# A four-layer transformer on one core: the second and third layer as one job of a sequence, with the orders planned anew

## The chip, the cores and the metric

The kernel runs on 1 core of one Trainium2 chip. The metric is the device time of one execution in microseconds (us). The core has five engines that work beside each other and wait for one another by semaphores: TensorE (PE, matmuls), VectorE (DVE), ScalarE (ACT), GpSimd (POOL) and SyncE (SP, here only the issuer of transfers).

## The reference, cut to what matters

Input x has 16 sequences of 256 tokens, 256 features, in float32. It passes through four layers, each with its own weights and its own modulation by a conditioning vector:

```
x = L0(x, cond, ctx)   # self-attention (rope, mask), cross-attention, mlp
x = L1(x, ctx, cond)   # cross-attention alone
x = L2(x, cond, ctx)   # self-attention, cross-attention, mlp
x = L3(x, cond, ctx)   # self-attention (rope), cross-attention, mlp
```

A block normalises x, modulates it, does its work and adds the result to x. Attention has 16 heads of 16 features; cross-attention looks at 77 context tokens. An mlp goes from 256 to 1024 features and back with a gelu between (tanh form in L0 and L2, erf form in L3). Sequences do not touch each other.

## The kernel before, in words

A *job* is one sequence in one entry of the list `LAYERS` (line 65). Before, the list has four entries: L0, L1, L2, L3, so 64 jobs. All 16 jobs of an entry come before those of the next (`JOBS`, line 97). That makes passes over the sequences: in between, x lies in a DRAM tensor, x_scratch. The step `stx` stores it at a job's end (line 1117), the step `ldx` loads it at the start of the same sequence's job in the next pass (line 1027) into one of two tiles x_in.

Six jobs are in flight (`SLOTS`, line 33). Each has its own tiles x, xhat (the normalised x) and xnT (its transpose). The rest is shared in small rings: 4 PSUM banks `gen`, 2 double banks `score`, 4 tiles of probabilities, 3 for cross-attention's keys and values, and so on. Weights lie in four areas A, B, C, M; an area is loaded anew (`ldw`) when the last job that uses it has finished. L1 and L3's self-attention share area C, whose query and output weights lie in the mask tiles maskk and maskq of L0: on PE, a matmul with `maskq,xnT` in these layers is the output projection, one with `xnT,maskk` the query projection, and `ctxT,w_kvC` L1's keys. The mlps of L0, L2 and L3 share area M (w_w1M for the up-projection, w_w2M for the down-projection).

A block is cut into steps, each of which belongs to one engine. In an attention block: `ln`, `rs`, `nx` (norm: DVE, POOL, DVE), `xT` (transpose on PE, line 1213), `xe` (ACT, line 1429), the projections `qkv` (PE, lines 1204 and 1238), splitting into a high and a low part and a trip through DRAM that lays queries and keys out (DVE, ACT, SP), the scores by rows `S` (PE, lines 1266 and 1280) whose row maxima `mr` DVE takes (line 1671), the scores by columns `ST` (PE, lines 1296 and 1302) whose exponentials `ex` ACT takes (line 1489), the weighing `W` (PE, line 1322), its copy (ACT), the sums' inverse `dv` and the division `nm` (DVE, POOL line 1531), `out` (PE, line 1204) and the residual `res` (DVE). An mlp has `up` (PE, line 1342), the gelu `ge` (ACT, line 1513) and `down` (PE, line 1351). The gelu and the exponential need different tables in ACT, which are loaded at each change between the two.

The order of every engine's steps is set before the program is built: `Program.run` plays the steps through with a table of costs and picks, for a free engine, the startable step with the smallest key

```
AGE * st.job - st.rank - STAY * (same tile shape on PE as the step before) - FIRST.get(st.name, 0.0)
```

so `FIRST` (line 106) holds for each kind of step by how much it is preferred, and `STAY` how much PE keeps to one shape of tile. The engines then run these orders as written; only semaphores hold them up.

Of the kernel before, what the change touches and what calls it, by code (L numbers as in the profile page):

```python
# [14 lines left out]
B, S, D = 16, 256, 256  # L15
# [34 lines left out]
class Block:  # L50
# [3 lines left out]
    def __init__(self, of, kind, area, eps, mod=None, rope=None, mask=False, gate=None, qk_bias=None, out_bias=False,  # L54
# [11 lines left out]
    [Block("L0", "self", "A", 1e-5, mod=0, rope=P, mask=True, gate=0),  # L66
     Block("L0", "cross", "B", 1e-5, mod=1, gate=1, mask=True, ctx="raw"),
     Block("L0", "mlp", "M", 1e-5, mod=2, gate=2, out_bias=True, gelu="tanh")],
    [Block("L1", "cross", "C", 1e-5, mod=3, qk_bias=0, out_bias=True, ctx="norm", ctx_mod=4, behind=(0, 0))],
    [Block("L2", "self", "A", 1e-6, mod=5, qk_bias=2, out_bias=True, gate=3),  # L70
     Block("L2", "cross", "B", 1e-6, qk_bias=4, out_bias=True, ctx="norm"),
     Block("L2", "mlp", "M", 1e-6, mod=6, gate=4, out_bias=True, gelu="tanh")],
    [Block("L3", "self", "C", 1e-5, mod=7, rope=S),
# [29 lines left out]
HOP = {"pe": 0.29, "act": 0.21, "dve": 0.14, "pool": 0.12, "sp": 0.1}  # L103
TABLE = 1.28
TRANSFERS = ("ldx", "ldc", "ldg", "stx", "zq", "sm", "sd", "sg", "sh", "ldw", "ph", "pw", "lh", "ll", "la", "ms")
FIRST = {"ce": 15.3, "dv": 0.7, "ex": -9.3, "ge": 5.3, "hi": 11.9, "ldc": 8.9, "ldg": 13.3, "ldx": 13.4, "lh": -6.3, "ln": -5.3, "lo": 0.5, "mr": 2.3, "out": 3.8, "ph": -2.2, "pv": -6.8, "pw": 2.6, "qkv": -6.1, "rp": -8.7, "rt": -6.9, "sd": -0.6, "stx": 4.2, "up": -1.9, "ve": -10.0, "xT": -2.5, "xe": 8.2, "zq": 13.4}
MARGIN, AGE, STAY = 1.4, 16, 4
ISSUE = {"ldw": 2.5, "la": 0.5, "ms": 0.4, "zq": 0.55, "lh": 1.27, "ll": 0.63, "sm": 0.56, "sd": 0.53, "sg": 1.08, "sh": 0.53}
TILES = {"S": "rows", "ST": "rows", "W": "columns"}
SWITCH = {("whole", "rows"): 0.095, ("rows", "whole"): 0.095, ("rows", "columns"): 0.095, ("columns", "rows"): 0.1,  # L110
# [114 lines left out]
class Program:  # L225
# [154 lines left out]
    def run(self):  # L380
# [45 lines left out]
        while left:  # L426
            started = False
            for eng in ENGINES:
# [3 lines left out]
                if not can:  # L432
                    continue
                st = min(can, key=lambda st: (AGE * st.job - st.rank - STAY * (eng == "pe" and TILES.get(st.name, "whole") == self.tiles) - FIRST.get(st.name, 0.0), 0))
                could[eng].remove(st)
# [1405 lines left out]
```

How the kernel before makes its waits and increments, by code:

```python
                @block.sync  # L711
# [9 lines left out]
                                sp.dma_start(dst, src).then_inc(w_loaded[st.blk.area], 16)  # L721
                        elif st.early:
                            buf = st.got["x_in"]
                            sp.dma_start(x_in[buf][:, :, :], a["x"][st.seq].rearrange("(c p) d -> p c d", p=P)).then_inc(x_loaded[buf], 16)
                    sp.dma_start(late_gates[:, :], a["gate_bias"][0, GATES_EARLY * D:N_GATE * D].partition_broadcast(B)).then_inc(late_bias_loaded, 16)
                    sp.wait_ge(hot_ready, 1)
                    sp.dma_start(zeros_dram, zero[:, :]).then_inc(hot_placed, 16)
                    for t in k_self:
                        sp.dma_start(t[0:P:4, :, :].bitcast(F32), hot[:, :, :]).then_inc(hot_placed, 16)
                    for t in k_cross:
                        sp.dma_start(t[0:P:4, :, :].bitcast(F32), hot[:, :, 0:CTXP]).then_inc(hot_placed, 16)
                    for i, late in enumerate(LATE):
                        if late.then is None:
                            dst, src = late_dma(i)
                            sp.dma_start(dst, src).then_inc(late_loaded[i], 16)
                    sp.wait_ge(hot_placed, 16 * (1 + OWN + CROSS))
                    sp.wait_ge(gates_ready, 2)
                    sp.dma_start(gates_dram[:, 0:GATES_EARLY * D], gates[:, :]).then_inc(gates_stored, 16)
                    sp.wait_ge(gates_stored, 16)
```

## Time and profile before

| what | value |
|---|---|
| median of 3 runs | 2713.38 us (2712.58 to 2728.46) |
| the profiled execution | 2724.64 us |
| its span, first to last instruction | 2722.9 us |
| mean granted clock of PE | 0.961 |
| PE busy | 2592.7 us (95%) |
| DVE busy | 1772.4 us (65%) |
| ACT busy | 1510.7 us (55%) |
| POOL busy | 658.4 us (24%) |

The span counts from the first to the last instruction of the profiled execution. Busy time is the union of an engine's instructions; PE's matmuls overlap each other, so the durations of single matmuls add up to more than it. The granted clock of a stretch is a mean: PE's clock has a full and a half level.

### The profile page before, as it was taken

Reading aid. Unit: us, or ns where it says so; the run is one execution under the profiler, and the core shown is the slowest. Engines: PE = TensorE matmul, PEld = TensorE weight load, DVE = VectorE, ACT = ScalarE, POOL = GpSimd, SP = SyncE. Lnnn points to the kernel's source line nnn. Section 1 sums busy time; section 2 is a strip of 40 time slices with the busy share of each in tenths; the row PEclk is TensorE's granted clock in tenths of the full one; section 3 lists DMA queues with packets and bytes.
Section 4 is the critical chain, followed back from the end, with each engine's and each line's share of the span. In section 5 each row is a group of like instructions: output and inputs, shape, how many; then the busy total and the mean of one; then the engine's idle time right before and its main releaser. Section 6 shows DMA issues by size and latency. Waiting matters only on the chain.

```text
span 2722.9 us, 55574 instructions
## 1 busy us (share of the span) xinstructions
PE 2592.7 (95%) x19774; PEld 1871.0 (69%) x19774; DVE 1772.4 (65%) x4435; ACT 1510.7 (55%) x2471; POOL 658.4 (24%) x650
## 2 busy tenths in 40 slices
PE   7789999999999999989999999999999999999987
PEld 5557777777776766656677777776776777777766
DVE  4467656755765565777675767675776777677741
ACT  1335566566565554445666666655655555655562
POOL 2013212212222222212222222222332232323220
PEclk9889999999999987888999999999999999999988
DMA  6344334334334454545343434343334343434310
GB/s 201 117 132 131 117 103 146 101 103 139 108 102 131 150 183 138 175 159 166 109 153 102 146 114 148 113 142 112 116 118 153 101 144 98 135 108 147 94 62 16
DMA packets 317577, 342.69 MB, mean 126 GB/s; under 512 B 90874, under 2 KB 208474, under 8 KB 316988
## 3 DMA queue, kind: packets, MB, share of 16 engines
q1 hardware_dynamic: 284860, 292.06, 34.5%
q10 hardware_dynamic: 32256, 47.07, 4.8%
q8 instruction: 165, 2.70, 0.4%
q14 instruction: 104, 0.85, 0.1%
q0 software_dynamic: 192, 0.01, 0.0%
HBM read 203.42 MB, written 118.31 MB: 118 GB/s over the span
## 4 chain that ended last, share of the span: by engine, by line
PE 76%; DVE 12%; SPq 3%; issue 3%; DMA 3%; ACT 2%; POOL 0%; ACTq 0%; DVEq 0%; POOLq 0%
PE gen L1342 12%; PE gen L1351 11%; PE gen L1238 11%; PE gen L1204 11%; PE gen L1322 10%; DVE row_max L1671 5%; PE score L1296 4%; PE score L1251 3%; PE score L1280 3%; PE score L1266 3%; PE score L1302 3%; PE gen L1213 3%; DVE xhat L1586 1%; DVE max_tok L1686 1%; DVE stats L1574 1%
## 5 line engine op out<-in xcount | busy, mean ns | idle before, releaser
L1489 ACT ACTIVATE probs<-score 128x1024 f32<-128x1024 f32 (+1 forms) x576 | 572.3, 1027 | 331.0 <-PE score L1296 216.1
L1671 DVE TENSOR_REDUCE row_max<-score 128x4 f32<-128x1024 f32 (+1 forms) x640 | 648.5, 1044 | 139.8 <-PE score L1280 95.6
L1342 PE MATMUL gen<-xnT,w_w1M 128*128 128x256 f32 x1536 | 374.3, 393 | 2.2 <-ACT xnT L1429 2.2
L1351 PE MATMUL gen<-w_w2M,hT 128*128 128x256 f32 x1536 | 354.7, 385 | 3.0 <-ACT hT L1513 3.0
L1342 PEld LDWEIGHTS gen<-xnT,w_w1M 128*128 128x128 f32 x1536 | 284.9, 193 | 65.1 <-issue 18.2
L1351 PEld LDWEIGHTS gen<-w_w2M,hT 128*128 128x128 f32 x1536 | 286.5, 191 | 56.9 <-issue 18.3
L1523 POOL TENSOR_TENSOR rstd<-var_eps,minus_half 128x2 f32<-128x2 f32 x160 | 112.4, 703 | 864.2 <-DVE var_eps L1580 863.9
L1531 POOL TENSOR_TENSOR xnT<-xnT,xhat 128x512 f32<-128x512 f32 x112 | 142.5, 1272 | 597.0 <-DVE xhat L1700 578.3
L1498 ACT COPY oT<-gen 128x512 f32<-128x512 f32 x224 | 132.0, 589 | 218.6 <-PE gen L1322 210.8
L1429 ACT ACTIVATE xnT<-gen,mod_all 128x256 f32<-128x256 f32 x288 | 147.0, 568 | 181.3 <-PE gen L1213 180.0
L1720 DVE TENSOR_TENSOR xhat<-gen,gate 128x256 f32<-128x256 f32 (+1 forms) x112 | 60.1, 537 | 228.0 <-PE gen L1351 154.8
L1322 PE MATMUL gen<-probs,v_self 128*32 128x256 f32 x3072 | 206.1, 386 | 0.1
L1513 ACT ACTIVATE hT<-gen,b_b 128x256 f32<-128x256 f32 x384 | 159.0, 473 | 79.2 <-PE gen L1342 78.2
L1266 PE MATMUL score<-k_self,q_stack 64*128 64x256 f32 x1536 | 185.2, 335 | 12.4 <-DVE row_max L1671 8.2
L1537 POOL TENSOR_TENSOR parts<-parts,sinT 128x512 f32<-128x512 f32 (+1 forms) x96 | 109.8, 1144 | 346.3 <-DVE parts L1615 346.3
L1296 PE MATMUL score<-q_stack,k_self 64*128 64x256 f32 x1536 | 183.5, 336 | 0.8 <-ACT probs L1489 0.7
L1280 PEld LDWEIGHTS score<-k_cross,q_stack 64*128 64x128 f32 x2048 | 143.0, 199 | 54.8 <-issue 54.3
L1266 PEld LDWEIGHTS score<-k_self,q_stack 64*128 64x128 f32 x1536 | 124.2, 188 | 80.6 <-issue 62.3
L1296 PEld LDWEIGHTS score<-q_stack,k_self 64*128 64x128 f32 x1536 | 122.8, 188 | 75.2 <-issue 56.9
L1280 PE MATMUL score<-k_cross,q_stack 64*128 64x78 f32 x2048 | 161.8, 291 | 9.4 <-DVE row_max L1671 8.5
L1322 PE MATMUL gen<-probs,v_cross 77*32 77x256 f32 x2048 | 165.8, 410 | 4.9 <-ACT probs L1489 2.6
L1513 ACT ACT_TABLE_LOAD x82 | 105.2, 1283 | 98.0 <-PE gen L1342 97.2
(160 smaller groups left out, 4131.0 us busy)
## 6 DMA issues: line engine op xcount, KB each, us to landing
q_stack<-parts_scratch SPq DMA_DIRECT2D x336, 256.0 KB
parts_scratch<-parts ACTq DMA_DIRECT2D x160, 256.0 KB, 2.5
parts_scratch<-parts SPq DMA_DIRECT2D x160, 256.0 KB, 2.6
k_self<-parts_scratch SPq DMA_DIRECT2D x144, 256.0 KB, 3.9
k_cross<-parts_scratch SPq DMA_DIRECT2D x192, 78.0 KB, 2.4
xnT<-oT SPq DMA_DIRECT2D x224, 64.0 KB, 1.8
x_scratch<-x SPq DMA_DIRECT2D x48, 256.0 KB, 3.3
x_in<-x_scratch SPq DMA_DIRECT2D x48, 256.0 KB, 2.8
```

Of the source, the lines that this page charges most:

```text
L1204: mm = pe.matmul(out, xT[:, fc], weight[:, fc, cols], start=fc == 0, stop=fc == FC - 1)
L1238: mm = pe.matmul(out[:, c, :], weight[:, fc, cols], xT[:, fc, :], start=fc == 0, stop=fc == FC - 1)
L1266: mm = pe.matmul(buf[:, t, c * S:c * S + S], queries[rows, column(u), c * P:c * P + P], keys[rows, column(u), :], start=not blk.mask, stop ...
L1280: mm = pe.matmul(buf[:, t, at_col:at_col + CTXP], queries[rows, column(2 * u + i), c * P:c * P + P], keys[rows, column(2 * u + i), :], sta ...
L1296: mm = pe.matmul(buf[:, t, kc * S:kc * S + S], keys[rows, column(u), kc * P:kc * P + P], queries[rows, column(u), :], start=not blk.mask, ...
L1322: mm = pe.matmul(pv[VW * i:VW * i + VW, within, :], value, e, start=kc == 0, stop=not blk.whole or kc == TC - 1, skip_group_check=True)
L1342: mm = pe.matmul(buf[:, i * S:i * S + S], w["M"]["w1"][:, fc, col:col + P], xnT[s][:, fc, :], start=fc == 0, stop=fc == FC - 1)
L1351: mm = pe.matmul(buf[:, 0:D], hT[:, j, c * P:c * P + P], w["M"]["w2"][:, j, :], start=j == 0, stop=j == FFC - 1)
L1429: ins = act.activation(out[:, fc, :], buf[:, fc * stride:fc * stride + width], ACT.Identity, bias=mod_all[:, st.seq, col + FC:col + FC + 1 ...
L1489: act.activation(probs[st.probs][0:keys, :, :], score[st.fill.buf][0:keys, :, :].rearrange("p a (r q) -> p (a r) q", r=2), ACT.Exp, bias=k ...
L1513: ins = act.activation(hT[:, 2 * j + i, :], gen[st.fill.buf][:, i * S:i * S + S], fn, bias=b1[:, 2 * j + i:2 * j + i + 1])
L1671: dve.tensor_reduce(dst, src, AX_X, ALU.max).then_inc(max_done[b], 1)
```

## The change

The list of layers now has three entries: L0, then L1's block followed by L2's three, then L3. So there are 48 jobs in three passes; a job of the middle entry has four blocks, and x stays in its slot's tile x from L1's residual to L2's norm. The 16 stores of x after L1 and the 16 loads before L2 are gone. L1's block is still the first of its job and reads x_in; L2's self-attention is now the second and reads and writes x in place. The constants `FIRST` and `STAY` have new values, by which the orders of all passes change.

```diff
-    [Block("L1", "cross", "C", 1e-5, mod=3, qk_bias=0, out_bias=True, ctx="norm", ctx_mod=4, behind=(0, 0))],
-    [Block("L2", "self", "A", 1e-6, mod=5, qk_bias=2, out_bias=True, gate=3),
+    [Block("L1", "cross", "C", 1e-5, mod=3, qk_bias=0, out_bias=True, ctx="norm", ctx_mod=4, behind=(0, 0)),
+     Block("L2", "self", "A", 1e-6, mod=5, qk_bias=2, out_bias=True, gate=3),
      Block("L2", "cross", "B", 1e-6, qk_bias=4, out_bias=True, ctx="norm"),
      Block("L2", "mlp", "M", 1e-6, mod=6, gate=4, out_bias=True, gelu="tanh")],
...
-FIRST = {"ce": 15.3, "dv": 0.7, "ex": -9.3, ... "ldx": 13.4, "lh": -6.3, "ln": -5.3, ... "rt": -6.9, "sd": -0.6, ...}
-MARGIN, AGE, STAY = 1.4, 16, 4
+FIRST = {"S": 3.5, "cT": -4.8, "ce": 22.1, "cl": 7.1, "down": -5.6, "dv": -0.2, "ex": -9.3, ... "ldx": 3.0, "lh": -8.4, "ll": -4.7, "ln": -1.1, ... "rt": -36.4, "sd": 1.9, ...}
+MARGIN, AGE, STAY = 1.4, 16, 3.7
```

Three places show what that does to PE's order. A row names the line, the tiles with their numbers (an xnT, xhat or x by its slot), the size written and how many such matmuls follow each other.

First, PE in the middle of L1 as it was. All rows are attention: projections, scores and weighings of L1's blocks in several slots.

```order
L1238 MATMUL gen3<-xnT1,maskk 128x256 x4
L1204 MATMUL gen2<-maskq,xnT2 128x256 x4
L1302 MATMUL score1<-q_stack0,k_cross0 77x256 x4
L1302 MATMUL score0<-q_stack0,k_cross0 77x256 x4
L1322 MATMUL gen0<-probs2,v_cross0 32x256 x4
L1280 MATMUL score1<-k_cross1,q_stack2 128x78 x8
L1280 MATMUL score0<-k_cross1,q_stack2 128x78 x8
L1322 MATMUL gen0<-probs3,v_cross0 32x256 x4
...
L1238 MATMUL gen1<-ctxT0,w_kvC 128x77 x4
```

In the middle pass of the changed order, PE goes from an up-projection of an mlp to its down-projections with L1's keys (`ctxT1,w_kvC`), L2's self-attention scores and an output projection of other jobs in between.

```order
L1238 MATMUL gen0<-ctxT1,w_kvC 128x77 x4
L1342 MATMUL gen1<-xnT3,w_w1M 128x256 x4
L1266 MATMUL score1<-k_self1,q_stack0 128x256 x4
L1266 MATMUL score0<-k_self1,q_stack0 128x256 x4
L1204 MATMUL gen3<-w_outA,xnT0 128x256 x4
...
L1351 MATMUL gen2<-w_w2M,hT 128x256 x8
```

With the numbers left out and equal rows merged, 336 rows in a row of the order before hold no mlp matmul (from L0's last down-projection to L2's first up-projection). In the changed order the longest such run has 62 rows, at the same place of the program.

Second, PE a little later in the same pass: L1's output projection in slot 2 (`maskq,xnT2`) is followed in the same slot by the transpose of L2's norm (`ident,xhat2`) and L2's query projection (`xnT2,w_qA`).

```order
L1204 MATMUL gen1<-maskq,xnT2 128x256 x4
L1266 MATMUL score0<-k_self1,q_stack0 128x256 x4
L1302 MATMUL score1<-q_stack1,k_cross1 77x256 x4
L1213 MATMUL gen3<-ident,xhat0 128x128 x4
L1204 MATMUL gen2<-w_kvC,ctxT1 77x256 x2
L1224 MATMUL gen0<-ident,ctx_in1 128x77 x2
...
L1213 MATMUL gen0<-ident,xhat3 128x128 x4
L1238 MATMUL gen3<-xnT0,w_qB 128x256 x4
L1238 MATMUL gen0<-xnT3,maskk 128x256 x4
L1213 MATMUL gen2<-ident,xhat2 128x128 x4
...
L1238 MATMUL gen3<-xnT2,w_qA 128x256 x4
```

Before, the output projection of L1 and the transpose of L2's norm of one sequence stood a whole pass apart.

Third, PE at the end of the program. The last job was in slot 3: its last weighing is followed at once by its output projection.

```order
L1351 MATMUL gen0<-w_w2M,hT 128x256 x8
L1322 MATMUL gen1<-probs1,v_cross0 32x256 x4
L1322 MATMUL gen2<-probs2,v_cross0 32x256 x4
L1322 MATMUL gen2<-probs3,v_cross0 32x256 x4
L1204 MATMUL gen3<-w_outA,xnT3 128x256 x4
L1213 MATMUL gen0<-ident,xhat3 128x128 x4
L1342 MATMUL gen1<-xnT3,w_w1M 128x256 x4
```

Now the last job is in slot 5, and both down-projections of the job before it stand between its last weighing and its output projection.

```order
L1322 MATMUL gen0<-probs2,v_cross2 32x256 x4
L1342 MATMUL gen1<-xnT4,w_w1M 128x256 x4
L1322 MATMUL gen0<-probs3,v_cross2 32x256 x4
L1351 MATMUL gen3<-w_w2M,hT 128x256 x8
L1351 MATMUL gen2<-w_w2M,hT 128x256 x8
L1204 MATMUL gen1<-w_outA,xnT5 128x256 x4
L1213 MATMUL gen0<-ident,xhat5 128x128 x4
```

What moved: two long matmul runs from before the last weighings to behind them. Over the whole program PE's order has 2620 rows before and 2667 now, ACT's has 164 table loads before and 176 now, and SP's has 48 stores to x_scratch before and 32 now.

## Rows read from the trace of the kernel before

**Rows 1.** The page: span, and busy time of each engine with its share.
```profile
span 2722.9 us, 55574 instructions
PE 2592.7 (95%) x19774; PEld 1871.0 (69%) x19774; DVE 1772.4 (65%) x4435; ACT 1510.7 (55%) x2471; POOL 658.4 (24%) x650
```

**Rows 2.** Stages: length, busy us (x) of PE, PEld, DVE, ACT, POOL; clock, DMA, GB/s.
```profile
0.00:840.00 840.00, 790.78 (x6352) 566.68 (x6352) 515.70 (x1204) 437.18 (x682) 180.28 (x174) 0.98 0.40 125
840.00:1360.00 520.00, 480.32 (x3525) 337.85 (x3526) 338.25 (x977) 277.41 (x490) 110.78 (x117) 0.88 0.49 153
1360.00:1800.00 440.00, 439.70 (x3360) 322.01 (x3359) 305.29 (x820) 282.58 (x448) 102.20 (x108) 1.00 0.41 131
...
1900.00:2600.00 700.00, 688.68 (x5255) 500.32 (x5253) 511.85 (x1171) 410.44 (x685) 221.15 (x211) 1.00 0.38 121
2600.00:2723.00 123.00, 97.21 (x559) 73.89 (x557) 35.47 (x99) 47.59 (x78) 16.18 (x15) 0.88 0.10 30
```

**Rows 3.** PE's timeline (start, us, what): L0's last down-projections, L2's first up-projection.
```profile
951.41 7.17 PE L1351 MATMUL gen<-w_w2M,hT 128*128 128x256 f32 x32
...
1325.16 1.99 PE L1342 MATMUL gen<-xnT,w_w1M 128*128 128x256 f32 x8
```

**Rows 4.** Stages again, the stretch from 840 us cut finer.
```profile
840.00:960.00 120.00, 113.44 (x745) 87.86 (x745) 64.08 (x195) 66.55 (x120) 26.36 (x29) 0.94 0.44 138
960.00:1330.00 370.00, 339.45 (x2582) 230.04 (x2581) 259.72 (x742) 187.56 (x340) 77.27 (x81) 0.85 0.53 166
```

**Rows 5.** PE's waits, 840 to 1360 us: total us, times, longest.
```profile
PE score L1280 <- DVE row_max L1671: 5.8, 5, 2.0
PE gen L1204 <- POOL xnT L1531: 5.6, 4, 1.9
```

**Rows 6.** The chain of waits (start, us, what): one up-projection run, two jobs of L2.
```profile
1601.44 3.67 PE gen L1342 x16
...
1646.33 3.66 PE gen L1342 x16
```

**Rows 7.** The page's DMA issues: KB each, median us to landing.
```profile
x_scratch<-x SPq DMA_DIRECT2D x48, 256.0 KB, 3.3
```

**Rows 8.** PE's timeline at the end of the program; in brackets the idle time before.
```profile
2684.52 1.50 PE L1322 MATMUL gen<-probs,v_cross 77*32 77x256 f32 x24
2693.02 3.78 PE L1204 MATMUL gen<-w_outA,xnT 128*128 128x256 f32 x8 [6.99 <-POOL xnT L1531]
2700.41 1.12 PE L1213 MATMUL gen<-ident,xhat 128*128 128x128 f32 x4 [3.62 <-DVE xhat L1586]
2702.64 8.78 PE L1342 MATMUL gen<-xnT,w_w1M 128*128 128x256 f32 x32 [1.11 <-ACT xnT L1429]
```

**Rows 9.** PE's timeline in L1; a start less the one before is a run's time.
```profile
903.92 0.70 PE L1302 MATMUL score<-q_stack,k_cross 64*77 64x256 f32 x8
904.55 0.66 PE L1213 MATMUL gen<-ident,xhat 128*128 128x128 f32 x4
905.04 1.89 PE L1238 MATMUL gen<-xnT,maskk 128*128 128x256 f32 x8
906.77 1.03 PE L1204 MATMUL gen<-w_kvC,ctxT 128*77 128x256 f32 x4
907.73 0.46 PE L1302 MATMUL score<-q_stack,k_cross 64*77 64x256 f32 x4
908.12 0.64 PE L1322 MATMUL gen<-probs,v_cross 77*32 77x256 f32 x8
```

**Rows 10.** ACT's groups: busy us, mean ns of one, idle before them and its releaser.
```profile
L1513 ACT ACT_TABLE_LOAD x82 | 105.2, 1283 | 98.0 <-PE gen L1342 97.2
```

**Rows 11.** ACT's timeline in L2: an activation, a table load, the next activation.
```profile
1605.15 0.84 ACT L1513 ACTIVATE hT<-gen,b_b 128x256 f32<-128x256 f32 x2 [0.91 <-PE gen L1342]
1606.01 1.28 ACT L1489 ACT_TABLE_LOAD   x1
1607.31 1.02 ACT L1489 ACTIVATE probs<-score 77x1024 f32<-77x1024 f32 x1
```

More of the change, by code:

```diff
@@ L105 @@
 TRANSFERS = ("ldx", "ldc", "ldg", "stx", "zq", "sm", "sd", "sg", "sh", "ldw", "ph", "pw", "lh", "ll", "la", "ms")
-FIRST = {"ce": 15.3, "dv": 0.7, "ex": -9.3, "ge": 5.3, "hi": 11.9, "ldc": 8.9, "ldg": 13.3, "ldx": 13.4, "lh": -6.3, "ln": -5.3, "lo": 0.5, "mr": 2.3, "out": 3.8, "ph": -2.2, "pv": -6.8, "pw": 2.6, "qkv": -6.1, "rp": -8.7, "rt": -6.9, "sd": -0.6, "stx": 4.2, "up": -1.9, "ve": -10.0, "xT": -2.5, "xe": 8.2, "zq": 13.4}
-MARGIN, AGE, STAY = 1.4, 16, 4
+FIRST = {"S": 3.5, "cT": -4.8, "ce": 22.1, "cl": 7.1, "down": -5.6, "dv": -0.2, "ex": -9.3, "ge": 5.3, "hi": 11.9, "ldc": 22.1, "ldg": 13.3, "ldx": 3.0, "lh": -8.4, "ll": -4.7, "ln": -1.1, "lo": 0.5, "mr": 2.3, "nm": -1.1, "nx": -3.0, "out": 1.1, "ph": -2.2, "pv": -6.8, "pw": 5.2, "qkv": -6.1, "rp": -8.7, "rs": 0.1, "rt": -36.4, "sd": 1.9, "sg": -4.5, "sh": 6.4, "sm": 0.6, "stx": 4.8, "up": -1.9, "ve": -17.0, "xT": -2.5, "xb": 0.3, "xe": 8.2, "zq": 13.4}
+MARGIN, AGE, STAY = 1.4, 16, 3.7
 ISSUE = {"ldw": 2.5, "la": 0.5, "ms": 0.4, "zq": 0.55, "lh": 1.27, "ll": 0.63, "sm": 0.56, "sd": 0.53, "sg": 1.08, "sh": 0.53}
```

## The prediction

> **What bounds the kernel now.** I read the page first: TensorE (PE) is busy 2592.7 of 2722.9 us, VectorE (DVE) 65% and ScalarE (ACT) 55% [rows 1]. So the matmuls set the time, and only two things can be won without taking matmuls away: PE's idle 130 us, and the time in which its clock is granted at the lower of its two levels, 1.2 instead of 2.4 GHz. Next I read the view by stages [rows 2]. The reader is to see that the loss has an address. From 1360 to 1800 us, the third layer (L2) alone, PE is busy 439.7 of 440 us at full clock: nothing is left there. From 1900 to 2600 us, the fourth layer (L3), it idles 11.3 of 700 us. From 840 to 1360 us, the end of L0, all of L1 and the start of L2, it idles 39.7 of 520 us and the mean granted clock is 0.88. A stretch with mean clock c loses about (1 - c) of its busy time, here 0.12 x 480 = 58 us. Together this stretch loses 97 us. The rest of the loss is at the start (49 us idle up to 840) and at the end (26 us idle after 2600, clock 0.88).
>
> Why just there? An mlp block is long matmuls with little DVE work, an attention block is short matmuls, each of which DVE must read. L1 has no mlp. The timeline shows L0's last down-projection at 951.4 + 7.2 = 958.6 us and L2's first up-projection at 1325.2 us [rows 3]: 367 us in which PE sees attention alone. The finer stage view has in it 370 - 339.5 = 30.5 us of idle time and a clock of 0.85, so 30.5 + 0.15 x 339.5 = 82 us of loss; 840 to 960 has 6.6 + 0.06 x 113.4 = 13 us [rows 4]. Per us of PE work at full clock DVE has 259.7 / (370 - 82) = 0.90 us to do there, against 305.3 / 439.7 = 0.69 in L2 alone and 511.9 / 688.7 = 0.74 in L3 [rows 2, 4]. The list of waits agrees: its longest entries end at DVE's row_max and at POOL's xnT, which comes behind DVE, and no single one of these is over 2 us [rows 5]. It is DVE's load and the chains through it, not one slow transfer.
>
> **The change part by part.** The matmuls stay the same in number and shape, and the floor with them. The third layer's pace is 44.9 us a sequence (one up-projection run starts at 1601.44, the same one of the next job at 1646.33) [rows 6].
>
> *The passes.* L1's 16 attention blocks no longer stand alone: most now stand between L2's mlps, as the first place in the order shows. On PE the run of order rows without an mlp falls from 336 to 62. What is left of the 97 us? I price three pieces. The 62 rows lose at the old rate: 62/336 x 82 = 15 us. Ahead of them the order now spreads L0's last two mlps in pieces among L1 and L2 attention, about 125 us of PE work by the durations of its steps; there is some mlp, but each new job's DVE-heavy part comes first. I take half the old rate, 0.5 x 82/288 x 125 = 18 us (288 is 370 - 82, the PE work in the old stretch). The lead-in keeps half of its 13 us: 6. Sum 39 us. The bounds are 0 (as between 1360 and 1800) and 97 (nothing gained). So the term is **-97 + 39 = -58**.
>
> *The mixed pass itself.* A job of L1 and L2 takes about 57 us of PE work, 44.9 and some 12 for L1's block. Its DVE work is 0.69 x 44.9 = 31 us for L2 and about 11 for L1: DVE's busy time from 840 to 1800 is 643.5 us [rows 2]; less 14.3 L2 jobs of 31 us and some 16 us for L0's last mlps, a sixteenth of the rest is 11.5. That is 42 us of 57, or 0.74, L3's ratio, so I charge L3's idle share, 1.6%, on the 740 us that are left of the pass: **+12**. Bounds: 0 as in L2, and the handover rival below.
>
> *x stays on chip.* 16 stores and 16 loads of 256 KB go; each took about 3 us to land [rows 7] and was issued far ahead, on transfer engines that are 41% busy between 1360 and 1800 [rows 2]. I cost this at nothing. New is a chain inside the job: L1's residual, L2's statistics, norm and transpose. At the kernel's end the same chain runs with nothing beside it, and PE waits 3.62 us for it [rows 8]. In the new order the PE work between the two ends is 3.2 us at the least and 6 in the middle, so it is covered if DVE comes to it at once; its misses are in the 12 us.
>
> *More changes of tile shape.* The PE order has 47 more rows (2620 to 2667). Two score steps in a row take 904.55 - 903.92 = 0.63 us, one alone 908.12 - 907.73 = 0.39 [rows 9]; twice one alone is 0.15 more than a pair. 47 x 0.15 = **+7**, bounds 0 and 47 x 0.39 = 18.
>
> *ScalarE's tables.* The ACT order has 176 table loads instead of 164. The rows have 1283 ns for one [rows 10], so 12 x 1.28 = 15 us more on an engine that is busy 282.6 of 440 us in its fullest stretch [rows 2]; covered, 0, upper bound 15. In the Trainium skill, the page "ScalarE: Activation LUTs", section "What ACT_TABLE_LOAD costs", speaks against such a change: functions should be grouped by table, since a switch costs a drain of about 1.38 us beside the load, 2.66 us in all, by which the upper bound would be 32 us. The trace doesn't show that drain: the load at 1606.01 starts 0.02 us after the activation before it ends, and the exponential starts 0.02 us after the load [rows 11].
>
> *The end.* The last job's output projection waits 6.99 us for POOL, since nothing stands between it and the last weighing, and then runs at half clock, 3.78 us instead of the 1.9 that eight such matmuls take [rows 8, 9]. The new order puts another job's two down-projections there, 7.2 us. What is late next is the 3.62 us chain behind it, which stays. **-9**, bounds 0 and -12.
>
> *The start.* The same first chains in another order; 0, bounds -8 and +8.
>
> **Sum.** -58 + 12 + 7 - 9 = -48 us against the profiled execution, 2724.6 us (span 2722.9), so 2676. That execution is 11 us above the median of the runs shown, 2713.4 us, from which I subtract the same 48: **2665 us**, 1.8% faster. About 1%, 27 us, is what a measurement of this kernel can tell from no change, so "faster" begins below 2686 and "slower" above 2740.
>
> **The rivals.** *The front costs nothing.* If L1's blocks find enough cover everywhere, the 39 and the 12 us vanish: 2614 us. For it: L2 alone loses 0.3 us in 440 though it has the same six jobs in flight. Against it: each new pass must begin with attention, and the first L2 mlp still waits for L0's last one to give its weights' place free.
>
> *The attention front is merely moved.* The order between L0's last and L2's first mlps is denser than before: L1 blocks and L2's self-attention blocks of several jobs together. If it loses all that the old stretch lost, 97 instead of 39, the time is 2665 + 58 = 2723, no change. For it: the self blocks have the longest row maxima. Against it: 62 rows instead of 336.
>
> *The handover stalls (slower).* Place: the 16 points where L2's first transpose waits for L1's residual, 3.2 to 6 us of PE work apart. If DVE has a queue of row maxima when the residual comes, PE waits the whole chain, 3.6 us, and what follows runs at half clock: after the last such wait the transpose took 1.12 us for the usual 0.49, and 8.78 for four up-projections of 1.83 each, together 2.1 more [rows 6, 8, 9]. 16 x 5.7 = 91 us more: 2756. It becomes slower than before by over 1% when 13 of the 16 miss entirely. Against it: the same chain stands between L2's blocks now, as close, and costs nothing there.
>
> That x is still sent through memory is excluded: the SP order has 32 stores to x_scratch instead of 48.
>
> **How the numbers follow.** Forecast 0.52 (own range 2640 to 2690), free front 0.17, moved front 0.22, handover 0.06, something unforeseen at start or in L3's new order 0.03. Range: 2610 takes in the free front with a better end, 2715 most of the way to the moved front; what lies outside is the handover, the upper part of the moved front and a little below, under 0.2. Faster: 0.95 of the forecast, the free front, a tenth of the moved front: 0.68. Slower: the handover and a little of the unforeseen: 0.07. Same: 0.25.
>
> **What would show it.** Right: the stage view of the new profile has no stretch after 1000 us with a clock below 0.95 except the end; the loss around 830 to 1000 us is 30 to 50 us; L3 begins some 50 us earlier; the last output projection no longer waits 7 us. Wrong: PE idle time spread evenly through the mixed pass with xhat as releaser (handover), or a stretch of 200 us at clock 0.85 after L0 (moved front). The prediction fails altogether if the new order of L0 or L3, where I charged nothing, loses tens of us.

## The result: 2.3% slower, and the profile after

The changed kernel takes **2781.1 us** in the median of 4 runs (2775.29 to 2784.6), the kernel before beside it 2712.98 us. The ratio is **1.0227, with a 95% interval of 1.0201 to 1.0254**: slower by 2.3%, where I forecast 1.8% faster. The profiled execution took 2780.23 us. Of the experiments below, one execution of e12 took 5956.53 us, where its other three took 2801 to 2810, and is left out of its ratio.

The first lines of its page, against [rows 1]: the span, and each engine's busy time with its share.

```profile
span 2778.3 us, 55538 instructions
PE 2617.4 (94%) x19774; PEld 1879.3 (68%) x19774; DVE 1783.1 (64%) x4435; ACT 1522.5 (55%) x2483; POOL 663.0 (24%) x650
```

PE runs the same 19774 matmuls. Of the 55.4 us by which the span grew, 30.7 are idle time of PE (160.9 instead of 130.2) and 24.7 are busy time for the same matmuls. The clock explains little of the 24.7: its mean is 0.960 against 0.961 before. Laid against the trace's clock records, PE is busy at the half level for 197.7 us instead of 186.1, which costs 5.8 us (half of the difference). The other 19 us are busy time that the same matmuls take at either level, as the profile models it; the part on tile shapes comes back to them.

Where? This is the view by stages of the changed kernel, PE alone: stretch, its length, PE's busy us (matmuls), mean granted clock, DMA share, GB/s.

```profile
300.00:830.00 530.00, 522.47 (x4275) 1.00 0.36 113
830.00:1210.00 380.00, 341.01 (x2406) 0.88 0.43 134
840.00:1360.00 520.00, 475.21 (x3440) 0.90 0.42 132
1210.00:1340.00 130.00, 125.87 (x976) 0.97 0.36 111
1340.00:1750.00 410.00, 383.75 (x2803) 0.92 0.37 118
1750.00:2000.00 250.00, 245.06 (x1921) 1.00 0.42 135
...
2655.00:2778.00 123.00, 103.71 (x643) 0.94 0.13 44
```

The row 840 to 1360 overlaps its neighbours; it stands there to be laid against [rows 2]. And the other stretches of the kernel before, which [rows 2] cut elsewhere:

```profile
300.00:830.00 530.00, 529.00 (x4345) 1.00 0.37 116
830.00:1210.00 380.00, 350.89 (x2548) 0.87 0.51 158
1210.00:1340.00 130.00, 121.16 (x954) 0.91 0.48 153
1340.00:1750.00 410.00, 407.82 (x3094) 1.00 0.40 127
1750.00:2000.00 250.00, 245.96 (x1910) 0.98 0.37 118
```

I read each row as one number, its **loss**: length less busy time times clock, the time in which PE did not work at full speed. The clock has two digits, so a loss is good to some 2 us. The stretches are the same times in both kernels, not exactly the same work.

| stretch, us | loss before | loss after |
|---|---|---|
| 300 to 830, L0 | 1 | 8 |
| 830 to 1210, the front of the middle pass | 75 | 80 |
| 1210 to 1340 | 20 | 8 |
| 1340 to 1750 | 2 | 57 |
| 1750 to 2000 | 9 | 5 |
| sum 830 to 2000 | 106 | 150 |
| the last 123 us | 37 | 25 |

So the front did not go away, and in the middle of the joined pass, where L2 alone had run without loss, there is a new hole of 57 us. The end got 12 us better. The differences add up to 39 of the 55 us. Most of the rest is no loss in this sense: it is the 19 us by which PE was busy longer at either level.

The list of PE's waits from 900 to 2000 us (engine and line, what released it; us in total, times, longest) shows what the hole is not:

```profile
PE score L1266 <- DVE row_max L1671: 11.4, 8, 6.8
PE gen L1213 <- DVE xhat L1586: 7.7, 8, 2.2
PE score L1302 <- DVE row_max L1671: 6.0, 7, 1.4
PE score L1302 <- ACT probs L1489: 5.8, 7, 2.6
PE score L1296 <- DVE row_max L1671: 4.3, 8, 2.1
```

No place stands out. The waits are for VectorE's maxima, its norm and ScalarE's exponentials alike, a few us each. The handover between L1 and L2, my slower rival, would have to show in the second row; 7.7 us in eight waits is not 91. In the hole alone, from 1340 to 1750 us, that row leads the list, but with 4.9 of the 26.2 us that PE idles there:

```profile
PE gen L1213 <- DVE xhat L1586: 4.9, 4, 2.2
PE score L1302 <- ACT probs L1489: 3.4, 3, 2.6
```

Most of these waits are not the handover's. With PE's matmuls counted off along the kernel's own order, the idle time just before the 16 transposes that follow L1's residual is 2.6 us in all.

### The profile page after: what moved, and what is told of

Its sections match the earlier page's. It is cut to its first block and busy times, and to the rows that moved or that the text cites. A ratio compares the mean times of both kernels' runs of the same rounds, so it can differ in the third digit from the quotient of the medians.

```text
span 2778.3 us, 55538 instructions
## 1 busy us (share of the span) xinstructions
PE 2617.4 (94%) x19774; PEld 1879.3 (68%) x19774; DVE 1783.1 (64%) x4435; ACT 1522.5 (55%) x2483; POOL 663.0 (24%) x650
## 5 line engine op out<-in xcount | busy, mean ns | idle before, releaser
L1720 DVE TENSOR_TENSOR xhat<-gen,gate 128x512 f32<-128x512 f32 (+1 forms) x112 | 59.6, 532 | 159.0 <-PE gen L1351 99.9
L1513 ACT ACT_TABLE_LOAD x88 | 112.9, 1283 | 75.2 <-PE gen L1342 74.2
```

Source lines behind the costliest of these rows:

```text
L1513: ins = act.activation(hT[:, 2 * j + i, :], gen[st.fill.buf][:, i * S:i * S + S], fn, bias=b1[:, 2 * j + i:2 * j + i + 1])
```

## The experiments

Two numbers stand beside each kernel: the ratio to the kernel before, measured on the same chip, and the *planned length*, which is what `Program.run` itself arrives at when it lays the orders out with its table of costs. It is no measurement, but it tells what the order's author could have known: 2611 us before, 2628 after. The planner itself has the joined form 17 us longer.

My theory after reading the trace was about **slots**. A job holds one of six slots from its first norm to its last residual. I followed this in the trace by counting PE's matmuls off along the kernel's own order: for sequences 4 to 11, from a job's first transpose to its last down-projection, an L1 job holds its slot 89 us and an L2 job 267; a joined job holds it 390 us. Six slots that are always full then finish a job every 65 us (64.8 measured over the same sequences), while by the terms of the prediction a job has 57 us of work for PE. This sum alone proves nothing: where the slots are full, the stay is always their number times the pace, whatever sets the pace. L2 before holds its slots 267 us, about six times its pace of 44.9 [rows 6], and loses nothing. So the number of slots had to be changed. The rivals: the new constants, VectorE's load, the cross-attention buffers.

**e1 and e2: form and constants apart.** e1 is the changed kernel with the old constants, e2 the kernel before with the new ones.

```diff
 e1, against the changed kernel:
-FIRST = {"S": 3.5, "cT": -4.8, "ce": 22.1, ...
-MARGIN, AGE, STAY = 1.4, 16, 3.7
+FIRST = {"ce": 15.3, "dv": 0.7, "ex": -9.3, ...
+MARGIN, AGE, STAY = 1.4, 16, 4
 e2, against the kernel before: the same lines the other way round
```

> The change alone, without its constants: second and third layers in one job, but the planner's constants (FIRST, AGE, STAY) of the kernel before. Slot theory (a joined job keeps one of the six slots about half as long again as a job of a single layer, so fewer jobs stand ready for TensorE, whatever the constants): slower than before, 2800 to 2860 us, with the loss in the pass of the joined jobs. Constants theory (the searched constants fit the plan's costs and not the chip): near my forecast, 2640 to 2720. VectorE theory: about the changed kernel's 2781, within 25.

> The constants alone: three-layer jobs as before (second and third layers apart, x through DRAM), with the changed kernel's constants. Slot theory: within 45 us of before, 2690 to 2760. Constants theory: as slow as the changed kernel, 2770 or more.

Measured: e1 2793.82 us, ratio 1.0269 (1.0235 to 1.0302), below the 2800 to 2860 that I had named for slots and inside the 25 us around 2781 named for VectorE, so e1 speaks against the constants and leaves these two. e2 2751.98 us, ratio 1.0111 (1.0079 to 1.0142). The form alone costs 2.7%; the new constants give 0.4 points back in the joined form, and cost the separate form 1.1%. So the form is the cause, and the constants are not its remedy: they shorten the joined plan by 51 us (2679 to 2628) and the kernel by about 11. The 7 us in L0 are theirs, though: from 300 to 830 us e1 loses 1 us like the kernel before, e2 14.

**e3: VectorE's load.** The changed kernel in its order, with the row maxima of self-attention over every second column.

```diff
-  src = score[b][:, :, :].rearrange("p h (c k) -> p h c k", c=TC)
+  src = score[b][:, :, :].rearrange("p h (c k) -> p h c k", c=TC)[:, :, :, 0:S:2]
```

> The changed kernel in the same order, but the row maxima of self attention read every second column only (that part of the computation is changed; it takes some 200 us off VectorE's 1783, about 70 of them in the pass of the joined jobs). VectorE theory (VectorE's load sets the pace of the joined pass): the stretches 830 to 1210 and 1340 to 1750 lose half as much, 2700 us or less. Slot theory: the order of TensorE is fixed and waits on the whole chain of a job, so it falls by 15 to 45 us, to 2735 to 2765.

Measured: 2758.62 us, ratio 1.0128 (1.0097 to 1.016), about 1.0 points or 27 us below the changed kernel. The page shows that the load did go:

```profile
span 2758.3 us, 55538 instructions
PE 2608.2 (95%) x19774; PEld 1874.6 (68%) x19774; DVE 1597.3 (58%) x4435; ACT 1521.6 (55%) x2483; POOL 662.5 (24%) x650
```

186 us less on VectorE bring 27. The hole from 1340 to 1750 shrinks from 57 to 43 us, the front from 80 to 71. That is the 15 to 45 us named for slots; the VectorE theory wanted half of both losses gone. VectorE is a part of each job's chain, not what sets the pace.

**e4 and e8: five slots, in either form.**

```diff
-SLOTS = 6
+SLOTS = 5
```

> The changed kernel with five slots instead of six. Slot theory: the pass of the joined jobs is bound by the jobs in flight, so a fifth fewer costs 100 to 200 us, 2880 to 2980, most of it between the end of the first layer and the start of the fourth. VectorE and constants theories: slots are not what runs out there, 2780 to 2825.

> The kernel before with five slots (its own constants). Slot theory: jobs of a single layer leave their slot sooner, so a slot fewer costs less than the 137 us that it cost the joined form in e4: 60 to 110, ratio 1.022 to 1.040. Rival (slots bind both forms alike): 1.045 or more.

Measured: e4 2920.16 us, ratio 1.0731 (1.0698 to 1.0763). e8 2867.29 us, ratio 1.055 (1.0521 to 1.058). A slot fewer costs the joined form some 137 us, as expected. In e4 a joined job holds its slot 350 us; over the whole pass jobs end 66.5 us apart, 59.1 in the changed kernel. The hole deepens:

```profile
1210.00:1340.00 130.00, 115.39 (x800) 0.89 0.37 114
1340.00:1750.00 410.00, 367.48 (x2658) 0.89 0.35 106
1750.00:2000.00 250.00, 229.70 (x1650) 0.92 0.40 125
```

But e8 went against me: the separate form loses 149 us with five slots, no less than the joined one. Slots bind both forms. Of the loss, 15 us more stand between 300 and 830, 46 more between 830 and 2000 (152 instead of 106), and most of the rest after 2000. The kernel before shows no loss in L2 and was near the edge: with five slots the same stretch loses 29 us instead of 2:

```profile
1340.00:1750.00 410.00, 392.91 (x2914) 0.97 0.41 128
```

**e5 and e11: the seventh slot, and what made room for it.** Both are e1 with three query buffers instead of four (which frees the memory for a slot) and three x buffers instead of two. e5 has seven slots, e11 six. A semaphore that nothing waits for is dropped for the third x buffer; so line numbers are one less in these kernels.

```diff
-SLOTS = 6
+SLOTS = 7          # e5 alone
-QUERIES = 4
+QUERIES = 3
-X_IN = 2
+X_IN = 3
...
-tables_ready = sem("tables_ready")
...
-act.copy(sinT[:, :], gen[2][:, S:2 * S]).then_inc(tables_ready, 1)
+act.copy(sinT[:, :], gen[2][:, S:2 * S])
```

> Joined jobs with the constants of the kernel before (as e1), and seven slots instead of six; to make room and lend the slots work, three query buffers instead of four and three x buffers instead of two. Slot theory: most of the 72 us that e1 lost against before comes back, 30 to 75 us below e1 (ratio to before 1.000 to 1.016). Rival (the joined jobs' own chain of waits is too long whatever the slots): within 20 us of e1, ratio 1.02 or more.

> e5 with six slots: three query buffers, three x buffers, constants of before. Slot theory: within 25 us of e1 (ratio 1.018 to 1.036), so that the seventh slot alone is worth 30 us or more of the 55 between e1 and e5. Rival (the third x buffer was it, which starts jobs earlier): ratio 1.013 or less.

Measured: e5 2739.2 us, ratio 1.0082 (1.005 to 1.0114); e11 2796.95 us, ratio 1.0303 (1.0271 to 1.0335). Between the two stands one slot, and 2.2 points or 60 us. The third x buffer, with one query buffer fewer, gives nothing over all (e11 against e1), though e11's first 300 us lose 46 instead of 64. The hole of the joined pass, first in e11, then in e5:

```profile
1340.00:1750.00 410.00, 382.78 (x2872) 0.93 0.38 117
1750.00:2000.00 250.00, 224.89 (x1646) 0.93 0.39 122
```

```profile
1340.00:1750.00 410.00, 392.36 (x3088) 0.99 0.41 129
1750.00:2000.00 250.00, 239.84 (x1797) 0.98 0.38 121
```

The losses are 54 and 41 us without the slot, 22 and 15 with it.

**e12: the cross-attention buffers.** A joined job has two cross-attentions, which share three pairs of key and value buffers; in the changed kernel's plan all three are taken for 82 to 97% of the time from 1000 to 1600 us, in slices of 200 us.

```diff
-CROSS = 3
+CROSS = 4
-QUERIES = 4
+QUERIES = 3
```

> e1 with four key and value buffers for cross attention instead of three, three query buffers instead of four to make room; six slots. Cross theory (a joined job has two cross attentions, and their three buffers are taken early and are what runs out): 40 us or more below e1, ratio 1.012 or less. Slot theory: within 25 us of e1, ratio 1.018 to 1.036.

Measured: ratio 1.0323 (1.0298 to 1.0348). Nothing gained. A ring that is nearly always full need not be the bound. The query buffer that had to go was not tried by itself; e5 gains with as few.

**e6, e7, e9, e10: four searches.** The constants were fitted to one form and six slots, so a fair comparison of forms searches anew in each. I did this alike for four cases, with as many trials for each: small random changes of `FIRST`, `AGE` and `STAY`, kept when the planned length did not grow. The seven-slot kernels have the buffers of e5. The diffs are the constants alone:

```diff
 e6, against e5:
-FIRST = {"ce": 15.3, "dv": 0.7, "ex": -9.3, ...
+FIRST = ...
```

> As e5, with constants searched for these buffers by the planner's own length, which falls from 2620 in e5 to 2551 (before: 2611). If the chip follows the plan with the 111 to 150 us that the kernels so far took more than their plans: 2660 to 2705, faster than before (ratio 0.98 to 0.995). If searched constants fit the plan's costs only (as in the changed kernel, where 51 planned us gave 11 to 13): 2715 to 2745.

> The layers apart as before, with the buffers of e6 and constants searched with as many trials (planned length 2558). Slot theory: the joined form has no handicap left with seven slots, so this is within 20 us of e6; if the joined form costs something of its own, this is 30 us or more below e6.

> Joined jobs, six slots and all buffers as in the changed kernel, constants searched with as many trials as e6 and e7 had (planned length 2615; the changed kernel 2628, e6 2551). Slot theory: the search can't find what the slots don't hold, so no faster than before, 2715 to 2780 (ratio 1.000 to 1.025). Search theory (e6 is fast for its search, not for its slots): 2690 or less, ratio 0.99 or less.

> The kernel before, its layers apart, six slots and all its buffers, constants searched with as many trials (planned length 2601, before 2611). With e6, e7 and e9 it makes four kernels of equal search: form by slots. If the plan's 10 us hold: 2695 to 2725. Slot theory: faster than e9 by 15 us or more, as the joined form is the one that six slots hold back.

Each cell is one search, and constants alone move these kernels by tens of us. So four more, from a second, independent search of each case:

> As e9 (joined, six slots, buffers of the changed kernel), constants from a second, independent search of as many trials (planned length 2622; e9 2615). If e9's 1.013 was the form's: 1.008 to 1.028. If it was that search's luck: 1.000 or less.

> As e10 (layers apart, six slots), second search (planned length 2603; e10 2601). Form by slots: 0.990 to 1.005, and 25 us or more faster than e13. Luck: no such distance.

> As e6 (joined, seven slots, three query and three x buffers), second search (planned length 2561; e6 2551). Form by slots: 0.963 to 0.980, no slower than e16 by more than 10 us. Luck (e6 a fortunate order): 0.985 or more, or 25 us slower than e16.

> As e7 (layers apart, seven slots), second search (planned length 2560; e7 2558). Form by slots: 0.970 to 0.985.

Measured, first and second search, with the loss from 830 to 2000 us worked out as above:

| form, slots | median us | ratio (95% interval) | planned | loss |
|---|---|---|---|---|
| apart, six: e10 | 2705.09 | 0.9948 (0.9932 to 0.9964) | 2601 | 89 |
| apart, six: e14 | 2712.02 | 0.9967 (0.9946 to 0.9988) | 2603 | 91 |
| joined, six: e9 | 2753.54 | 1.0127 (1.0101 to 1.0153) | 2615 | 103 |
| joined, six: e13 | 2774.93 | 1.0195 (1.0161 to 1.0229) | 2622 | 137 |
| apart, seven: e7 | 2660.64 | 0.9783 (0.974 to 0.9827) | 2558 | 90 |
| apart, seven: e16 | 2646.44 | 0.9734 (0.9705 to 0.9763) | 2560 | 89 |
| joined, seven: e6 | 2622.12 | 0.9643 (0.961 to 0.9675) | 2551 | 53 |
| joined, seven: e15 | 2642.15 | 0.9707 (0.9671 to 0.9743) | 2561 | 51 |

With six slots the joined form is 48 and 63 us slower than the separate one. With seven it is 38 and 4 us faster; of these only the first is outside the intervals. Read the other way, the seventh slot with its buffers gives the joined form 131 and 133 us and the separate one 44 and 66. That the handicap goes with the slot and its buffers is shown twice, and e5 against e11 shows it for the slot alone; that joining is a clear gain in the whole time at seven slots is not. In its own stretch it is: 52 us of loss instead of 90, in both searches. The whole time shows less of it, since the joined kernels are also busy longer at either level of the clock: 9 us in e6 against e7, 20 in e15 against e16.

Two expectations missed. e6 is 38 us faster than the range that the plan gave it, and e7 is 38 us slower than e6, where the slot theory had them within 20. The other six lie where the slot theory had them.

Two kernels show the stretch, e16 with the layers apart,

```profile
830.00:1210.00 380.00, 345.47 (x2657) 0.91 0.55 169
1210.00:1340.00 130.00, 122.97 (x964) 0.91 0.46 141
1340.00:1750.00 410.00, 407.13 (x3121) 1.00 0.40 127
1750.00:2000.00 250.00, 247.64 (x1925) 1.00 0.43 138
```

and e15, joined:

```profile
830.00:1210.00 380.00, 345.90 (x2656) 0.96 0.49 152
1210.00:1340.00 130.00, 130.00 (x1030) 1.00 0.40 125
1340.00:1750.00 410.00, 409.15 (x3253) 1.00 0.45 140
1750.00:2000.00 250.00, 247.38 (x1904) 1.00 0.42 132
```

In the first the front loses 66 + 18 us, then next to nothing, as in the kernel before. In the second the front loses 48, and from 1210 to 2000 us only 4. This is the picture that I had forecast for the change, and it takes seven slots.

**e6 beats both kernels**: 2622.12 us (2612.2 to 2626.71), 3.6% faster than before. Its page:

```profile
span 2610.4 us, 55470 instructions
PE 2525.6 (97%) x19774; PEld 1840.9 (71%) x19774; DVE 1792.3 (69%) x4435; ACT 1436.0 (55%) x2419; POOL 662.8 (25%) x650
```

PE idles 84.8 us and is busy 67 us less than before for the same matmuls. Not all of it is the joined pass: of the loss, the first 300 us have 40 instead of 63 and the middle 53 instead of 106, and the rest of the gain lies in L3 and the end.

## Why the prediction was wrong, step by step

- **The passes (-58).** This step failed nearly whole. I left 39 of 97 us of loss on 840 to 1360 us; 92 stand there (44.8 idle and a clock of 0.90), so the term is -5. I priced the front by which blocks stand there. The slots are a part of what I left out: one more takes the stretch 830 to 1210 from 71 to 56 us (e11, e5). The order is another part: e6 and e15, with seven slots and searched constants, lose 38 and 48 us, and the two searches with six slots 54 and 77 (e9, e13). It is not simply that jobs stay too long: L0's last two jobs hold their slots 298 and 342 us instead of 216 and 200, but in e15 308 and 372. VectorE's load, by which I had explained the old front, is little of it: with 186 us less (e3) the stretch loses 71 instead of 80. "The attention front is merely moved" was nearest for this piece.
- **The mixed pass itself (+12).** This is the step that failed outright, and no rival of mine had it: 57 us from 1340 to 1750 instead of 12 over the whole pass, and a clock of 0.92 where I had named 0.95 as a sign. I reasoned that VectorE has 0.74 us of work per us of PE, as in L3, so the pass would run like L3. But VectorE's load doesn't set it (e3), nor do the constants (e1) or the cross buffers (e12); a slot more takes most of it away (e5 against e11), a slot fewer deepens it (e4). What I took for evidence was the sentence that L2 alone "loses 0.3 us in 440 though it has the same six jobs in flight". No loss told me nothing of the margin: with a slot fewer the same stretch loses 29 us (e8). The number of jobs in flight is not in my sum at all.
- **Handover (the slower rival, 91).** Wrong too: 7.7 us of waits for xhat in 1100 us, and 2.6 us of idle time at the 16 handovers. The right sign stood behind the wrong mechanism.
- **x stays on chip (0).** Nothing in the profile after speaks against it. The list of PE's waits in the middle pass names no transfer of x.
- **Tile shapes (+7).** Too small, and probably the 19 us of busy time that the clock doesn't explain. I counted rows of the order, 47 more. What I had priced is a change of the tile's shape (the 128\*128 or 64\*77 in PE's rows) from one matmul to the next, and of these the trace has 1995 instead of 1907, 88 more; at my 0.15 us that is 13. Over all 18 kernels, PE's busy time with the half-level part counted half runs from 2485 to 2523 us, and a straight-line fit to it gives 0.15 us for each change of shape and 0.10 for each of PE's idle gaps (144 before, 192 after); it misses by 8 us at most. That is a fit: no run changed the shapes alone.
- **Table loads (0).** Not tested apart. The loads are 176, as the order said; the rows have 175 of them, with the same 1283 ns:

```profile
L1513 ACT ACT_TABLE_LOAD x88 | 112.9, 1283 | 75.2 <-PE gen L1342 74.2
L1489 ACT ACT_TABLE_LOAD x87 | 111.6, 1283 | 3.7 <-ACT parts L1479 1.3 <-ACT parts L1468 0.9
```

- **The end (-9).** Right: -12. PE's timeline of the end (start, us, what; in brackets the idle time before), against [rows 8] (the wait and the half clock of the output projection are 8.8 of the 12 us):

```profile
2743.26 7.14 PE L1351 MATMUL gen<-w_w2M,hT 128*128 128x256 f32 x32 [1.72 <-ACT hT L1513]
2750.30 1.99 PE L1204 MATMUL gen<-w_outA,xnT 128*128 128x256 f32 x8
2755.92 1.12 PE L1213 MATMUL gen<-ident,xhat 128*128 128x128 f32 x4 [3.62 <-DVE xhat L1586]
```

The last output projection waits for nothing and runs at full clock; the 3.62 us behind it stayed, as said.
- **L0 and the start (0).** The start is the same, 63 us of loss. L0 lost 7 us by the new constants; I had named L0 as a place where I charged nothing, and it is no tens of us.

In the Trainium skill, the page "Perfetto Trace Analysis", section "Identifying Performance Opportunities", says that consistent bubbles on the engine that should be saturated can mean that there isn't enough on-chip memory for the next tile, by the number or size of its buffers. Here the cause was of that kind, with e5 against e11 as the measurement. The bubbles did not look consistent, though: the waits in the list are spread over many places. That fits an order laid out in advance around the slots that there were, but no run shows that this is the reason.

**What stays open.** Why joined jobs need more slots isn't settled. That a joined job stays 390 us where its two parts apart stay 89 + 267 = 356 doesn't answer it, since a stay follows the pace and the number of slots: 350 us with five (e4), 437 with seven (e5). The comparison of forms and slots shows that a slot removes the effect, not which wait inside the job makes it. Nor is it shown how much of the separate form's gain at seven slots (from 0.995 to 0.978 and 0.973) is the slot's and how much the third x buffer's; in the joined form e11 shows nothing for the buffers. And the planned length orders neighbours badly (51 planned us gave 11 between e1 and the changed kernel, 69 gave 117 between e5 and e6): the plan doesn't know the clock.

## What to carry to other kernels

When work is fused into longer jobs, give the number of jobs in flight a term of its own, before counting what the fusion saves; the saved transfers were off the path here, and the slots were not. A long stay in a slot is no evidence by itself, since full slots make every job stay for their number times the pace. A stage without loss is no proof of slack: one run with a buffer fewer tells how near the edge it is. In a program whose order is laid out in advance, a missing buffer need not show as a wait of its own (it didn't here), so it has to be tested by changing its number. And time that the busiest engine spends busy is to be split too, into what its clock explains and what it doesn't.

## What the runs showed of the hardware

Idle time of PE went with a second loss, by the clock. Over kernels with the same 19774 matmuls, PE was busy 2526 us beside 85 idle (e6), 2593 beside 130 (before), 2617 beside 161 (after), 2663 beside 252 (e4). Of the busy time, 59, 186, 198 and 280 us stand at the half level. From e6 to e4 that is 167 us of idle time and 137 of busy time; 111 of the 137 are the lower clock (half of 221 us), and 26 are busy time at either level. It isn't a fixed rate: e5 idles 160 us, as much as the changed kernel, and is busy 2576, its mean granted clock 0.973 against 0.960.
